# Shared steps as turns of the experts' loop, with the rest of the up and gate weights packed: a one-core kernel of a mixture-of-experts layer

## What is computed

```python
x = x + tanh(g_xattn) * expert_forward(layernorm(x), w, ctx)     # first block, quantized
h = layernorm(x)                                                  # 2048 tokens x 512
scores = softmax(h @ gate_w.T); topk_w, topk_idx = top_k(scores, 2)
buf[e, pos] = h[token]                     # 16 experts, room for 256 tokens each
g = silu(einsum('ech,ehi->eci', buf, w_gate)); u = einsum('ech,ehi->eci', buf, w_up)   # i = 352
expert_out = einsum('eci,eih->ech', g * u, w_down)
y = sum over the two choices of expert_out[expert, pos] * topk_w
sh = (silu(h @ ws_gate) * (h @ ws_up)) @ ws_down                  # 704 wide
x = x + tanh(g_ffn) * (y + sh)
```

## Time and profile before

| | us |
|---|---|
| median of 3 runs (604.15 to 605.62) | 604.43 |
| the profiled execution | 607.08 |
| its span, first to last instruction | 605.1 |
| PE busy in the span | 554.5 |
| DVE, ACT, POOL busy | 412.9, 311.2, 166.8 |

### The profile page before, as it was taken

How to read it: one execution, slowest core, us unless ns; L and a number is a source line. 1 busy time by engine, 2 the same in 40 slices (tenths; PEclk the granted TensorE clock), 3 DMA queues, 4 the chain that set the end, 5 groups by cost and what they waited for, 6 DMA issues and landing times.

```text
span 605.1 us, 10166 instructions
## 1 busy us (share of the span) xinstructions
PE 554.5 (92%) x3855; PEld 471.5 (78%) x3863; DVE 412.9 (68%) x752; ACT 311.2 (51%) x472; POOL 166.8 (28%) x187
## 2 busy tenths in 40 slices
PE   7878879999999999999899999999999999729996
PEld 4435439777877888788799999999999999719895
DVE  4668999997998767774856656666656656105485
ACT  2285975777278354336465566665565565101211
POOL 2335782520231021032223322222222003740500
...
GB/s 270 382 97 2 36 139 1 36 70 70 2 35 1 1 166 1 118 38 352 170 201 230 265 225 226 212 223 252 247 248 243 233 219 122 205 159 36 209 98 77
DMA packets 45891, 89.52 MB, mean 148 GB/s; under 512 B 4304, under 2 KB 24784, under 8 KB 44832
## 3 DMA queue, kind: packets, MB, share of 16 engines
...
...
## 4 chain that ended last, share of the span: by engine, by line
PE 64%; DVE 20%; ACT 6%; issue 6%; POOL 3%; another core or an unknown queue 1%; DVEq 0%; ACTq 0%; POOLq 0%
PE ps_gu L1816 12%; PE ps_gu L1818 11%; PE ps_gu L1817 11%; PE ps_d L1816 6%; PE ps_d L1818 6%; PE ps_d L1817 6%; PE ps_a L2070 3%; PE ps_gu L1858 2%; POOL w L473 2%; PE ps_d L1837 1%; DVE bn_b L1071 1%; ACT y L742 1%; DVE x L1293 1%; DVE w_max_a L1200 1%; PE ps_a L1931 1%
## 5 line engine op out<-in xcount | busy, mean ns | idle before, releaser
L1816 PE MATMUL ps_gu<-ex_xhi,w_hi 128*128 128x256 f32 (+1 forms) x528 | 151.8, 287 | 5.5 <-issue 4.0
L1817 PE MATMUL ps_gu<-ex_xlo,w_hi 128*128 128x256 f32 (+1 forms) x528 | 149.7, 284 | 6.4 <-issue 6.4
L1818 PE MATMUL ps_gu<-ex_xhi,w_lo 128*128 128x256 f32 (+1 forms) x528 | 149.3, 283 | 1.6 <-issue 1.5
L1816 PEld LDWEIGHTS ps_gu<-ex_xhi,w_hi 128*128 128x128 f32 (+1 forms) x528 | 95.9, 182 | 9.7 <-issue 7.7
L1817 PEld LDWEIGHTS ps_gu<-ex_xlo,w_hi 128*128 128x128 f32 (+1 forms) x528 | 95.8, 181 | 7.1 <-issue 5.6
L1818 PEld LDWEIGHTS ps_gu<-ex_xhi,w_lo 128*128 128x128 f32 (+1 forms) x528 | 96.1, 182 | 4.9 <-issue 4.7
L974 ACT ACTIVATE ex_silu<-ps_gu 128x256 f32<-128x256 f32 (+1 forms) x66 | 24.8, 376 | 99.7 <-PE ps_gu L1818 69.2
L1816 PE MATMUL ps_gu<-xt_hi,sw_hi 128*128 128x256 f32 x220 | 64.7, 294 | 1.4 <-DVE sh_hid L1396 1.4
L1681 DVE TENSOR_TENSOR ex_hid<-ex_silu,ps_gu 128x256 f32<-128x256 f32 (+1 forms) x66 | 27.6, 418 | 53.9 <-ACT ex_silu L974 53.3
L1817 PE MATMUL ps_gu<-xt_lo,sw_hi 128*128 128x256 f32 x220 | 62.1, 282 | 0.0
L1818 PE MATMUL ps_gu<-xt_hi,sw_lo 128*128 128x256 f32 x220 | 62.1, 282 | 0.0
...
## 6 DMA issues: line engine op xcount, KB each, us to landing
...
```

Source lines behind the costliest of these rows:

```text
L1816: pe.matmul(dst, a_hi, b_hi, start=start, stop=False)
L1817: pe.matmul(dst, a_hi, b_lo, start=False, stop=False)
L1818: return pe.matmul(dst, a_lo, b_hi, start=False, stop=stop)
```

## The change

**Packing.** The last 96 columns of gate and of up are laid out anew. `w_hi`/`w_lo` keep the first 256 columns; `wa_hi`/`wa_lo` hold, side by side, the 96 of gate and the last 32 of up (128 columns), and `wb` the first 64 columns of up's rest twice: high part, then rest. Chunk 2 becomes 4 x 3 matmuls with `wa` and 8 with `wb` (128 wide by the tokens' high part, 64 wide by their rest): 20 for 24. The up half of chunk 2 then lies in three places of `ps_gu`, so ACT copies 32 and 64 rows of it into a new tile `ex_up`, and DVE adds 64 rows to it, with a wait of its own (`ex_added`), before `ex_hid`. ACT's one split becomes four instructions, DVE's two become five. In DVE's order the second `weights_gu` now stands ahead of `tokens`.

**The tail as turns.** PE's loop runs to turn 20 and one more turn stands behind it. Each of the six steps turns, splits and sums its own tokens: five token turns on PE, ACT and DVE behind expert 15 instead of two, six loads by SP instead of three, and six `shared_rows` (the last is `last_rows`) instead of three. ACT and DVE keep their tails written out, in a new order. PE waits for tokens on one semaphore pair `xg_ready` everywhere; for the gathered ones SP raises it once `xg_in` has come (`rows_landed`).

```diff
-    w_hi[0] = place(cur, "w_hi0", [P, 2, C, I], R32)
+    w_hi[0] = place(cur, "w_hi0", [P, 2, C, 2 * P], R32)
+    wa_hi[0] = place(cur, "wa_hi0", [P, C, P], R32)
+    wb[0] = place(cur, "wb0", [P, C, P], R32)
...
+    OWN, REST = 2 * P, I - 2 * P
+    PAIR = P - REST
+    FOLDED = REST - PAIR
... SP
-            def load_tokens(t):
-                b, h = TAIL[t]
-                sp.wait_ge(ex_xt, E - 1 + t)
-                sp.dma_start(xg[t % 2][:], x2n_v[b][:, HALF * h:HALF * (h + 1), :]).then_inc(xf_in[t % 2], 16)
+            def load_tokens(e):
+                b, h = TAIL[(e - E) // 2]
+                sp.wait_ge(ex_xt, e - 1)
+                sp.dma_start(xg[e % 2][:], x2n_v[b][:, HALF * h:HALF * (h + 1), :]).then_inc(xg_ready[e % 2], 16)
+            def rows_landed(k, q):
+                sp.wait_ge(xg_in[q], 32 * k + 32)
+                sp.sem_inc(xg_ready[q], 16)
... ACT
-                act.activation(w_hi[q][:], raw_gu[q][:], ACT.Copy).then_inc(ex_whi, 1)
+                act.activation(w_hi[q][:], raw_gu[q][:, :, :, 0:OWN], ACT.Copy)
+                act.activation(wa_hi[q][:, :, 0:REST], raw_gu[q][:, 0, :, OWN:I], ACT.Copy)
+                act.activation(wa_hi[q][:, :, REST:P], raw_gu[q][:, 1, :, OWN + FOLDED:I], ACT.Copy)
+                last = act.activation(wb[q][:, :, 0:FOLDED], raw_gu[q][:, 1, :, OWN:OWN + FOLDED], ACT.Copy)
...
+                if m == M - 1:
+                    act.activation(ex_up[FOLDED:REST, :], ps_gu[REST:P, (q + m) % 2, 0:CAP], ACT.Copy)
+                    act.activation(ex_up[0:FOLDED, :], ps_gu[FOLDED:P, (q + m) % 2, CAP:2 * CAP], ACT.Copy)
                 act.activation(ex_silu[0:k, (q + m) % 2, :], ps_gu[0:k, (q + m) % 2, 0:CAP], ACT.Silu).then_inc(ex_sg, 1)
... DVE
+                up = ps_gu[0:k, (q + m) % 2, CAP:2 * CAP]
+                if m == M - 1:
+                    dve.tensor_tensor(ex_up[0:FOLDED, :], ex_up[0:FOLDED, :], up[0:FOLDED], ALU.add).then_inc(ex_added, 1)
+                    dve.wait_ge(ex_added, e + 1)
+                    up = ex_up[0:REST, :]
...
                 hidden(e, q, 1)
+                weights_gu(e + 1, 1 - q, 1)
                 tokens(e + 1, 1 - q)
-                weights_gu(e + 1, 1 - q, 1)
                 hidden(e, q, 2)
... PE
+                    for c in range(C):
+                        three(ps_gu[:, u, 0:CAP], wa_hi[q][:, c, :], wa_lo[q][:, c, :], ex_xhi[q][:, c, :], ex_xlo[q][:, c, :],
+                              c == 0, c == C - 1)
+                    folded = ps_gu[:, u, CAP:2 * CAP]
+                    for c in range(C):
+                        last = pe.matmul(folded, wb[q][:, c, :], ex_xhi[q][:, c, :], start=(c == 0), stop=(c == C - 1))
+                        if c < C - 1:
+                            pe.matmul(folded[0:FOLDED], wb[q][:, c, 0:FOLDED], ex_xlo[q][:, c, :], start=False, stop=False)
...
-            with pe.Fori(1, E // 2 - 1) as r:
+            with pe.Fori(1, NE // 2 - 1) as r:
                 step(2 * r + 1, r, 1)
                 step(2 * r + 2, r + 1, 0)
-            step(E - 1, E // 2 - 1, 1)
-            for t in range(len(TAIL)):
-                for w in range(2):
-                    tail_up(t, w, 0)
...
+            step(NE - 1, NE // 2 - 1, 1, last=True)
+            down(NE - 1, 1, 2)
```

More of the change, by code:

```diff
@@ L154, in flamingo_block @@
     cur = [region]
-    raw_gu, raw_d, w_hi, w_lo, wd_hi, wd_lo, ex_xhi, ex_xlo, eo, xg = ([None, None] for _ in range(10))
-    w_hi[0] = place(cur, "w_hi0", [P, 2, C, I], R32)
-    xg[1] = place(cur, "xg1", [P, HALF, D])
+    raw_gu, raw_d, w_hi, w_lo, wa_hi, wa_lo, wb, wd_hi, wd_lo, ex_xhi, ex_xlo, eo, xg = ([None, None] for _ in range(13))
+    w_hi[0] = place(cur, "w_hi0", [P, 2, C, 2 * P], R32)
+    wa_hi[0] = place(cur, "wa_hi0", [P, C, P], R32)
+    wb[0] = place(cur, "wb0", [P, C, P], R32)
     raw0 = cur[0]
@@ L392, in _ @@
             load_shared(E + 1, 1)
-            load_tokens(1)
+            load_tokens(E + 1)
             store_eo(E - 2, 0)
             store_eo(E - 1, 1)
-            load_tokens(2)
+            for e in range(E + 2, NE):
+                load_tokens(e)
             with sp.Fori(0, B - 1) as b:
@@ L1013, in _ @@
             hidden(E, 0, 1, False)
+            tokens(E + 1, 1)
             hidden(E, 0, 2, False)
@@ L1016, in _ @@
             for e in range(E + 1, NE):
-                t = (e - E) // 2 + 1
                 hidden(e, e % 2, 0, False)
                 hidden(e, e % 2, 1, False)
-                if e % 2 and t < len(TAIL):
-                    tokens(E + t, t % 2)
+                if e + 1 < NE:
+                    tokens(e + 1, (e + 1) % 2)
                 hidden(e, e % 2, 2, False)
@@ L1788, in _ @@
             hidden(E + 3, 1, 0)
+            shared_rows(E + 2)
+            hidden(E + 3, 1, 1)
+            tokens(E + 4, 0)
             add_rows(1, 0)
-            hidden(E + 3, 1, 1)
-            tokens(E + 2, 0)
             hidden(E + 3, 1, 2)
@@ L1794, in _ @@
             hidden(E + 4, 0, 0)
-            shared_rows(1)
+            shared_rows(E + 3)
             hidden(E + 4, 0, 1)
-            dve.wait_ge(ex_eo, E + 1)
+            tokens(E + 5, 1)
+            dve.wait_ge(ex_eo, E + 2)
             add_rows(2, 0)
@@ L1801, in _ @@
             hidden(E + 5, 1, 0)
-            dve.wait_ge(ex_eo, E + 2)
+            shared_rows(E + 4)
+            hidden(E + 5, 1, 1)
+            dve.wait_ge(ex_eo, E + 5)
             add_last(0)
-            hidden(E + 5, 1, 1)
             add_last(1)
@@ L2419, in step @@
                 down(e, q, 0, evicted)
-                turn_tokens(e + 1, k + q, 1 - q)
+                if not last:
+                    turn_tokens(e + 1, k + q, 1 - q)
                 up(e, q, 2, first)
```

127 lines of the change are left out of this document (61 added, 66 removed).

## The result

| | us |
|---|---|
| before, median of 13 runs (603.21 to 607.67) | 605.84 |
| changed kernel, median of 13 runs (608.98 to 615.89) | 613.03 |
| ratio, with 95% interval | 1.0116 (1.0092 to 1.0141) |
| span of the profiled execution, before and after | 605.1 and 611.0 |

A forecast was written before the change was run, and what follows sets the result against it. PE was taken to bound the kernel, full in expert turns but stalled in the tail. 604.43 - 4.3 (experts) + 2.1 (tail), stall unchanged, gave 602.2 us, by itself 599 to 606.2; overall range 578 to 610.

The forecast's parts named there:

- The mechanism of the expert turn: Expert loop: four fewer matmuls save PE 0.47 us, the later chain into down 0 gives back 0.2; net 0.27 a turn.
- The two copies: ACT's copies ahead of chunk 2's silu, in the chain into down 0: 0.29 us each, +0.58 together.
- Rival B: Chain into down 0 late by 0.7 us, more than packing saves; 610 us (606.2 to 616), chance 0.23 with C.
- sixteen turns of 0.27: All expert turns: net packing gain of 0.27 us times 16, -4.3 us (0 to -7.5).
- The tail's own cost: Six shared steps behind the experts: -1.9 + 1.7 + 1.2 + 1.1 = +2.1 us (0 to +4).
- the hold: Tail, from the turning in E + 1 to that in E + 3: PE stalls with POOL's fetches, about 20.5 us lost.
- The turnings and the packed matmuls: Tail on PE: two more turnings cost +1.7 us, four packed steps save -1.9.
- the last chain: Tail's end: copies, addition and their wait put the last hidden rest +1.1 us later, at least +0.6.
- DVE's order: Tail: row sums behind the tokens' rest delay chunk 2's chain; down 2 late 0.4 us in three steps, +1.2.
- I take the hold as it is, at 0: Tail stall of 20.5 us taken as unchanged by the loop: 0 for the sum, -21.5 us the other end.
- rival A: The hold goes with the straight code or is broken up by the new order: 581 us (577 to 588), chance 0.27.
- if the hold moves to another turning and is longer: Tail: sign that the forecast is wrong at once; five turnings stand there now. No size given.

The follow-up runs named there:

- after_again: The changed kernel as it is, run and traced a second time: 613.06 us, ratio 1.0125 against the kernel before.
- spaced kernel before: Kernel before, POOL's fetches of experts' rows spaced by waits on PE's up chunks (two per chunk, last 8 three): 584.60 us, ratio 0.9648.
- spaced changed one: Changed kernel with POOL's fetches spaced by waits on PE's up chunks: 584.63 us (1.0007) on the fifth chip, 587.47 (0.9688) on another.
- packing alone: Kernel before with only the packing, tail of before and dense fetches: 600.27 us, ratio 0.9912.
- the tail as turns alone: Kernel before with only the tail as turns, chunk 2 kept at 24 matmuls, dense fetches: 615.14 us, ratio 1.0151.
- plain fetches: Kernel before with POOL's 32 fetches replaced by SP's plain transfers of consecutive rows (not the token's rows): 584.70 us, ratio 0.9653.

## Why the prediction was wrong, point by point

**The mechanism of the expert turn was right, its size nearly.** Forecast: 0.47 saved, 0.2 given back, 13.33 us. The narrow matmuls cost 0.117 as assumed. The turn is 13.41 (`ex_hlo` at 409.26 and down 0 at 409.32): 0.19 gained, 0.28 given back. The two copies were put at 0.29 each and take 0.39. Rival B's point of decision, 0.34, was not reached.

**First failure: sixteen turns of 0.27.** The sum took a turn from the middle and multiplied it by 16. The first turns are not such turns: there DVE was already late before. PE waited for it 1.27 us ahead of turn 1's up 0 and 1.39 us ahead of its down 0, and in the changed kernel 2.38 and 1.80. So what packing saved on PE was lost in the waits, what it added on DVE counted, and in the profiled execution PE's clock fell behind the second wait (302 to 304 us at 0.50). That made +2.3 in place of -0.5 for two turns; in `after_again`, with the same wait and the clock at 1.00, +0.5. The thirteen turns from turn 2 gave -2.7 in place of -3.5. The experts and the first turns together are worth -0.4 in the profiled execution and -2.1 in the other, not -4.3.

**The tail's own cost was right.** Forecast +2.1. Without the hold, from the turning in turn 15 to the end, it is 583.6 - 492.67 = 90.93 us in the spaced kernel before and 584.6 - 491.14 = 93.46 in the spaced changed one: +2.5. This stretch also holds step E and the packing of E + 1, which the sum left to the hold; with them the forecast is 2.1 + 0.87 - 0.94 = 2.0. The turnings and the packed matmuls cancel as said; the last chain costs 1.66 - 0.43 = 1.2 us more, as said (+1.1). DVE's order, put at +1.2, is 1.05 in the traces and not to be told in the medians.

**Second failure, the large one: "I take the hold as it is, at 0".** For the long hold that was right within the few us by which it varies (46.88 and 47.28 us; 46.50 in `after_again`, 44.59 in packing alone, 48.81 in the tail as turns alone), and rival A is refuted twice: the tail ran in a loop and the hold stayed, and with plain or spaced fetches it went in straight code too. But the step read the hold as a block of lost time that ends with POOL's last fetch and swallows what comes before. The second stretch is what that left out. In the traces, from the turning in E + 3 to the last down product: before 32.28, spaced 31.08, so 1.2 us of hold; changed 38.75, spaced 32.83, so 5.9. The difference, 4.7, and the tail's own 1.75 are the +6.47 of the table. That this stretch of dense fetches takes them is shown by spacing it alone.

Why it costs more than before is shown only in part. The stretch starts when DVE's sums of batch 0 are done, and these stand later in the turn. Where it holds PE, ACT has its report 1.0 to 1.8 us behind the end of the last fetch, so where in the turn the fetches end sets when PE can go on: they end 5.5 us behind the turning before and 8.2 in the changed kernel, with the report at 7.25 and 9.21; in the tail as turns alone it is 7.5, with the report at 8.85. The prediction had the order of DVE's sums and used it only on down 2's slack. The chain, longer by 1.2 us, adds to it in the changed kernel but is not needed: the tail as turns alone loses as much in that step without it, since PE's clock was at 0.65 and then 0.50 in the 8 us from 578 us on. And the place alone does not explain it: in packing alone the fetches end 7.1 us behind the turning, and PE is not held.

**What the text said would show it wrong** did: "if the hold moves to another turning and is longer". It had no price there. With the measured 4.7 us the sum would have been 604.43 - 4.3 + 2.1 + 4.7 = 606.9, and with the measured first turns and experts (-0.4 for -4.3) 610.8.

The Trainium skill, page "Runtime: NRT & Kernel Launch", section "Instruction fetch mechanics", warns of a stall where a taken branch leads to code outside the window that was fetched ahead. No such stall shows for this loop of two turns: in the experts its turns are 13.42 us with PE busy for 13.42, and in the tail, spaced, its steps take 13.16 to 13.65 us. Whether its code lies in that window no run shows.

## What stays open

Why a dense stream of POOL's fetches holds back PE's reports is not shown. The Trainium skill, page "DMA: Bandwidth & Descriptors", section "SWDGE vs HWDGE vs iDMA", says that GpSimd writes the descriptors of its own transfers into rings in SBUF and that SP's transfers don't touch that path. That fits the plain fetches; the page says nothing of PE, and no run here tells descriptors from any other part of POOL's path. Nor is it known why one chip of five is free of the hold; the changed kernel with dense fetches was not run on that chip, so that the change costs nothing there is inferred from its spaced form (1.0007). Why the second stretch did not hold packing alone at all, though it held the tail as turns alone on the same chip, was not tried either; one execution of each was traced. It is also open why PE's clock falls behind the same wait in one execution and not in another.
